# The second layer's small products moved from two quarters of TensorE to all four, with the values scaled ahead

## The reference, cut to what matters

```python
q = q / (norm(q) + EPS);  k = k / (norm(k) + EPS)          # per head, 64 wide
def step(s, inp):                                           # s: 64 x 64 per image and head
    qt, kt, vt, at, bt = inp
    s = s * at[..., None]
    u = einsum('bhd,bhdv->bhv', kt, s)
    s = s + bt * (kt[..., None] * (vt - u)[..., None, :])
    out = einsum('bhdv,bhd->bhv', s, qt)
y = y * rsqrt(mean(y * y, axis=-1) + EPS) * head_norm_w     # per head
```

## Time and profile before

| | |
|---|---|
| median of 3 runs | 722.4 us (719.88 to 723.09) |
| the profiled execution | 720.78 us, its span 719.0 us |
| PE busy | 633.8 us (88%) |
| DVE, ACT, POOL busy | 331.9, 268.5, 143.8 us |
| granted PE clock, mean | 0.938 |

### The profile page before, as it was taken

How to read it: one execution, slowest core, us unless ns; L and a number is a source line. 1 busy time by engine, 2 the same in 40 slices (tenths; PEclk the granted TensorE clock), 3 DMA queues, 4 the chain that set the end, 5 groups by cost and what they waited for, 6 DMA issues and landing times.

```text
span 719.0 us, 20213 instructions
## 1 busy us (share of the span) xinstructions
PE 633.8 (88%) x9154; PEld 468.0 (65%) x9154; DVE 331.9 (46%) x519; ACT 268.5 (37%) x536; POOL 143.8 (20%) x125
## 2 busy tenths in 40 slices
PE   8976497883899997679999998889999999999997
PEld 5654495682799996465566555665599966555553
DVE  0495835730011110374777778769636752411311
ACT  0353232210323232125566665457644533111223
POOL 9101020013000001712445445600043200000000
PEclk9987678985999999599999999999999999999999
DMA  9200000008998870100000020100000070000001
GB/s 316 106 0 2 4 3 2 1 5 303 406 346 312 337 277 29 52 0 24 26 26 26 27 83 20 45 4 0 2 4 5 5 293 1 1 0 1 0 1 45
DMA packets 20229, 56.38 MB, mean 78 GB/s; under 512 B 4272, under 2 KB 13104, under 8 KB 15792
## 3 DMA queue, kind: packets, MB, share of 16 engines
q1 hardware_dynamic: 19376, 53.00, 20.1%
q0 software_dynamic: 768, 2.10, 0.9%
HBM read 49.57 MB, written 5.52 MB: 77 GB/s over the span
## 4 chain that ended last, share of the span: by engine, by line
PE 70%; DVE 15%; issue 4%; ACT 4%; DMA 3%; POOL 2%; SPq 2%; DVEq 0%; ACTq 0%; POOLq 0%
PE PS L1461 8%; PE PS L1429 6%; PE PS L1501 6%; PE PS L1418 6%; PE PS L1597 6%; PE PS L610 4%; PE PS L1627 3%; PE PS L568 3%; PE PS L1604 3%; PE PS L600 3%; PE PS L578 3%; PE PS L589 3%; PE PS L1310 2%; PE PS L1324 2%; PE PS L249 2%
## 5 line engine op out<-in xcount | busy, mean ns | idle before, releaser
L1461 PE MATMUL PS<-Y,arena 128*128 128x392 f32 x192 | 75.1, 521 | 3.9 <-ACT Y L1190 3.9
L1501 PEld LDWEIGHTS PS<-arena 64*49 64x49 f32 x3584 | 50.8, 124 | 36.6 <-issue 22.2
L1501 PE MATMUL PS<-arena 64*49 64x48 f32 (+2 forms) x3584 | 57.3, 213 | 10.3 <-DVE arena L1749 5.7
L1418 PE MATMUL PS<-arena 128*128 128x128 f32 x448 | 54.8, 283 | 4.0 <-DMA arena<-in_moe_b 3.4
L1418 PEld LDWEIGHTS PS<-arena 128*128 128x128 f32 x448 | 54.2, 199 | 5.6 <-DMA arena<-in_moe_b 4.0
L1744 DVE COPY_PREDICATED arena<-msk,PS 128x768 f32<-128x768 int32 x24 | 44.9, 1870 | 27.3 <-PE PS L1501 27.3
L1184 ACT ACTIVATE arena<-PS,arena 128x128 f32<-128x128 f32 x112 | 31.8, 369 | 64.9 <-PE PS L1418 64.9
L1122 POOL TENSOR_TENSOR arena<-arena 128x384 f32<-128x384 f32 (+1 forms) x32 | 37.7, 1179 | 83.2 <-PE PS L1501 79.5
L1429 PE MATMUL PS<-arena 128*128 128x256 f32 x224 | 50.5, 379 | 0.0
L1461 PEld LDWEIGHTS PS<-Y,arena 128*128 128x128 f32 x192 | 33.9, 192 | 23.9 <-ACT Y L1190 4.2
L392 POOL TENSOR_TENSOR arena<-arena,work 128x512 f32<-128x512 f32 x20 | 25.4, 1270 | 114.0 <-DVE work L700 114.0
(11 more groups left out here) (226 smaller groups left out, 1133.9 us busy)
## 6 DMA issues: line engine op xcount, KB each, us to landing
arena<-in_moe_w SPq DMA_DIRECT2D x28, 1024.0 KB, 6.3
arena<-in_qka_w SPq DMA_DIRECT2D x8, 384.0 KB, 3.0
arena<-in_patches SPq DMA_DIRECT2D x6, 392.0 KB, 5.7
arena<-in_ff_w SPq DMA_DIRECT2D x1, 2048.0 KB, 7.7
arena<-in_ffn_w SPq DMA_DIRECT2D x2, 1024.0 KB, 12.6
by_expert<-arena SPq DMA_DIRECT2D x1, 1792.0 KB, 11.2
arena<-in_moe_b SPq DMA_DIRECT2D x14, 128.0 KB, 7.4
arena<-by_expert SPq DMA_DIRECT2D x14, 128.0 KB, 5.8
```

The lines of the kernel that those rows point to most:

```text
L1418: m = nc.tensor.matmul(PS[:, 4 + 2 * (j % 2) + f // 4, (f % 4) * P:(f % 4 + 1) * P], MW1[j % NW][:, k, f * P:(f + 1) * P], XT[:, j % 2, k] ...
L1461: m = nc.tensor.matmul(bank(i % 3), GW[g % 2][:, k, u // 2], half(Y[:, k], u % 2), start=(k == 0), stop=(k == KT - 1))
L1501: m = nc.tensor.matmul(o, K[r, b, :], v, start=True, stop=True)
```

## The change

Six things change:

1. Layer 2 (`PARTS = 2`): for odd pairs the matrices A, PT and U of an image lie on the other half of the partitions than its values. `small` writes them there (`c_`), `pe_rows` and `act_out` follow. A small product of an odd pair thus goes through a quarter of PE whose rows are one half and whose columns are the other, and a product of all 16 walks over all four quarters (`product`). Layer 1 keeps `PARTS = 1` and its two quarters.
2. In both layers a product now takes two banks at once (even pairs in one, odd pairs in the other), so each of the four has one buffer of two banks instead of two of one.
3. The values are multiplied by the key length ahead, head by head, on POOL (L395 of the changed kernel), when all values are stored. Then z is subtracted by DVE straight out of PSUM (L727), and POOL's subtraction and DVE's multiplication fall away.
4. The scaling of y goes from DVE to POOL (L399).
5. ACT masks only the second block of A; POOL clears the first block (L389).
6. `pe_rows` of layer 2 uses 64x49 quarters too, 8 rows in a group instead of 4; the squares, sums and roots come an iteration later.

```diff
-            def pool_apply(self, pool):
-
+            def pool_apply(self, pool, values_kept):
+
+                self.wait(pool, "turned_in", self.totals()["turned_in"])
+                nc.gpsimd.memset(self.Am[:, :, 0:BL], 0.0).then_inc(self.s["a_cleared"], 1)
+                self.wait(pool, "lengths", self.n_lengths)
+                pool.wait_ge(*values_kept)
                 for h in range(self.nh):
-                    self.wait(pool, "z_kept", h + 1)
                     w = self.W[:, :, h * DH:(h + 1) * DH]
-                    nc.gpsimd.tensor_tensor(w, w, self.ZT[h % 2], ALU.subtract).then_inc(self.s["w_kept"], 1)
+                    key = root[:, self.S + h * BP:self.S + (h + 1) * BP].unsqueeze(2).broadcast_to([P, BP, DH])
+                    nc.gpsimd.tensor_tensor(w, w, key, ALU.mult).then_inc(self.s["w_scaled"], 1)
+                for j in range(self.nh // 2):
+                    self.wait(pool, "y_inv", j + 1)
+                    y = self.y(j)
+                    nc.gpsimd.tensor_tensor(y, y, self.sums(y_var, j).unsqueeze(3).broadcast_to([P, BP, 2, DH]),
+                                            ALU.mult).then_inc(self.s["y_done"], 1)
...
+            def product(self, i, operands, back=False):
+
+                for pair in range(0, BP, 2):
+                    for b in (pair, pair + 1):
+                        for cc in range(2):
+                            there = (cc + b) % 2 if self.PARTS == 2 else cc
+                            r, o = (there, cc) if back else (cc, there)
+                            lhsT, rhs = operands(self.part(r), b)
+                            m = nc.tensor.matmul(
+                                PS[self.part(o), 2 * i + b % 2, (b // 2) * DH:(b // 2 + 1) * DH], lhsT, rhs,
+                                start=True, stop=True)
+                return m
...
                     if h < self.nh:
-                        if h >= 2:
-                            self.wait(pe, "d1_kept", h - 1)
-                        for b in range(BP):
-                            for cc in range(2):
-                                r = self.part(cc)
-                                m = nc.tensor.matmul(PS[r, h % 2, b * DH:(b + 1) * DH], self.U[r, h, b, :],
-                                                     self.W[r, b, h * DH:(h + 1) * DH], start=True, stop=True)
-                        m.then_inc(self.s["d1_mm"], 1)
+                        self.wait(pe, "w_scaled", h + 1)
+                        if h:
+                            self.wait(pe, "d1_kept", h)
+                        self.product(0, lambda r, b: (self.U[r, h, b, :], self.W[r, b, h * DH:(h + 1) * DH])) \
+                            .then_inc(self.s["d1_mm"], 1)
...
-                        nc.vector.tensor_tensor(
-                            self.ZT[h % 2], PS[:, 2 + h % 2, :].rearrange("p (b v) -> p b v", b=BP),
-                            inv_k[:, h * BP:(h + 1) * BP].unsqueeze(2).broadcast_to([P, BP, DH]),
-                            ALU.mult).then_inc(self.s["z_kept"], 1)
+                        nc.vector.tensor_tensor(self.head(h), self.head(h), self.result(1), ALU.subtract) \
+                            .then_inc(self.s["w_kept"], 1)
...
                         for b in (2 * pair, 2 * pair + 1):
-                            o = PS[TP * (b % 2):TP * (b % 2) + T, pb + hd]
+                            c_ = (b + pair) % 2
+                            o = PS[TP * c_:TP * c_ + T, pb + hd]
...
-            delta1.pool_apply(pool)
+            delta1.pool_apply(pool, (v1_kept, 2 * BP))
```

More of the change, by code:

```diff
@@ L516, in act_mask @@
                 self.wait(act, "turned_in", self.totals()["turned_in"])
-                nc.scalar.activation(self.Am, self.Am, ACT.Copy, scale=c("first")).then_inc(self.s["a_masked"], 1)
+                second = self.Am[:, :, BL:T]
+                nc.scalar.activation(second, second, ACT.Copy, scale=c("first")).then_inc(self.s["a_masked"], 1)
             def act_out(self, act, g):
@@ L557, in pe_apply @@
                 self.wait(pe, "a_masked", 1)
+                self.wait(pe, "a_cleared", 1)
                 for i in range(self.nh + 5):
@@ L573, in pe_apply @@
                         self.wait(pe, "d1_kept", h + 1)
-                        if h >= 2:
-                            self.wait(pe, "z_kept", h - 1)
-                        for b in range(BP):
-                            for cc in range(2):
-                                m = nc.tensor.matmul(PS[self.part(cc), 2 + h % 2, b * DH:(b + 1) * DH],
-                                                     self.A[self.part(cc), h, b, :],
-                                                     self.D[self.part(cc), h, b, :], start=True, stop=True)
-                        m.then_inc(self.s["z_mm"], 1)
+                        if h:
+                            self.wait(pe, "w_kept", h)
+                        self.product(1, lambda r, b: (self.A[r, h, b, :], self.D[r, h, b, :]), True) \
+                            .then_inc(self.s["z_mm"], 1)
                     h = i - 3
@@ L584, in pe_apply @@
                         self.wait(pe, "w_kept", h + 1)
-                        self.kept(pe, "delta", h - 2)
-                        for b in range(BP):
-                            for cc in range(2):
-                                r = self.part(cc)
-                                m = nc.tensor.matmul(PS[r, 4 + h % 2, b * DH:(b + 1) * DH],
-                                                     self.U[r, h, b, :], self.W[r, b, h * DH:(h + 1) * DH],
-                                                     start=True, stop=True)
-                        m.then_inc(self.s["delta_mm"], 1)
+                        self.kept(pe, "delta", h - 1)
+                        self.product(2, lambda r, b: (self.U[r, h, b, :], self.W[r, b, h * DH:(h + 1) * DH])) \
+                            .then_inc(self.s["delta_mm"], 1)
                     h = i - 5
@@ L595, in pe_apply @@
                         self.kept(pe, "delta", h)
-                        self.kept(pe, "out", h - 2)
-                        for b in range(BP):
-                            for cc in range(2):
-                                r = self.part(cc)
-                                m = nc.tensor.matmul(PS[r, 6 + h % 2, b * DH:(b + 1) * DH],
-                                                     self.PT[r, h, b, :], self.D[r, h, b, :], start=True, stop=True)
-                        m.then_inc(self.s["out_mm"], 1)
+                        self.kept(pe, "out", h - 1)
+                        self.product(3, lambda r, b: (self.PT[r, h, b, :], self.D[r, h, b, :]), True) \
+                            .then_inc(self.s["out_mm"], 1)
                     if 0 <= i - self.nh - 1 < self.EARLY:
```

118 lines of the change are left out of this document (62 added, 56 removed).

## The result

The changed kernel takes 751.0 us (median of 4 runs, 748.16 to 753.38) against 722.4; the ratio is 1.039, 95% interval 1.0354 to 1.0425. The forecast was 717, with a range up to 726. The changed kernel's profiled execution has a span of 751.5 us against 719.0.

The account below looks back on a forecast made before the run. The prediction took PE's products to bound layer 2's apply stage, DVE's dependent instructions the solve stages and hand-offs layer 1's apply stage. -24.0 + 9.8 + 3.6 + 6.1 - 0.6 = -5.1 us gave 717 us, range 704 to 726.

Parts of the forecast that it names:

- What four quarters give: Layer 2's products: 32 records on four quarters of PE take 0.49 us in place of 0.89.
- PE then needs 8 x 0.49 = 3.9 us: Layer 2's apply stage: PE's time for two heads, so that DVE binds and PE sees 4.1 instead of 7.1.
- -24.0: Layer 2's apply stage: forecast change in us, 39.7 in place of 63.7.
- The third rival: Layer 2's products: quarters take turns at the PSUM banks, a product stays at 0.89, 743 us; chance 0.06.
- Rows of A: Layer 2's `pe_rows` behind the last mask: four groups of 64 records, 0.8 us each, and fewer DVE instructions, -0.6 us.
- POOL's clear: Clearing of A's first block: masks and clears were to hide behind the solve chains, at no cost.
- Values scaled ahead, layer 2: End of layer 2's solve chain: POOL and DVE shut each other out for ten DVE instructions, +9.8 us.
- Layer 1: Beginning of layer 1's solve chain: POOL's four multiplications hold DVE up, +3.6 us, bounds 0 and 4.4.
- Layer 1's apply stage: Lost second buffers, POOL's scaling of y and a longer half clock: +6.1 us, bounds 4 and 9.
- DVE's 4.0 to 4.4 us for two heads: Layer 2's apply stage: DVE's work for two heads, which was to bind once the products were faster.
- the slower rival: Layer 2's apply stage: rings of single buffers bind, two heads take 5.4 instead of 4.1, 726 us; chance 0.17.

Follow-up runs that it names:

- the later scaling: Changed kernel, but POOL multiplies the values only after the solve chain in both layers, and ACT masks all of A with no clear by POOL: 737.2 us.
- the half kernel: Changed kernel, but each of layer 2's four products of a head issues only half of its small products: 728.9 us.

## Why the prediction was wrong

- **The step that failed** is "What four quarters give" and what rests on it, "PE then needs 8 x 0.49 = 3.9 us". The duration was right: a product takes 0.50 us inside a burst, and at 15.9 ns a record nothing shows of banks that take turns. The pace was wrong. The step took the array to be all that PE waits for, and left out the supply of instructions. I took the pace from 64 records, half of one packet, and used it for 2048 matmul records in a row. In steady state two heads take 7.0 to 7.6 us, not 4.1; that is the 26.5 us between -24.0 and +2.5. The third rival has the outcome (no gain in the stage, 743 us, chance 0.06), but by banks that take turns, so it would have been right by luck. The trace of the kernel before could have warned me: from 537 us on its iterations take 3.73 to 4.00 us where four products of 0.89 are 3.57, and each pause in them ends 1.2 to 1.6 us after a packet of the instruction queue has landed.
- **Rows of A** failed by the price, "0.8 us each" against 1.9 for a group of 64, and by the count: all six groups, not four, stand behind the last masked product. The price was carried over from other small products; here PE takes four records in 0.119 us without a gap, so it isn't the supply, and the cause of this pace stays open. That is 5.4 of the 7.7; 2.25 are POOL's clear, of which I wrote that it hides. The two make this step the second largest miss, 8.3 us.
- **Values scaled ahead, layer 2**: the mechanism was right, shown by the later scaling. The size was 7.2 for 9.8: one turn costs DVE 0.7 us, not 0.95, since the durations of the ten instructions add up to 11.5 us instead of 4.3. **Layer 1**: the first d1 came 1.8 later against 3.6 forecast, and scaling later gave 2.2 back. POOL's four multiplications take 4.03 us, 1.0 each where I had 1.27.
- **Layer 1's apply stage**: +7.0 for +6.1. Nearly all of it is the single buffers (6.7 back with two). POOL's scaling of y takes 1.9, not 2.5, and matters by less than 1 us here.
- **DVE's 4.0 to 4.4 us for two heads** was right (3.98 in the kernel with half the products), but never came to bind in the changed kernel.
- **Rivals**: the slower rival (rings in layer 2) has the right side and the wrong mechanism; the half kernel rules it out as the main cause. Single buffers alone do cost there too: with two quarters 70.8 us against 64.6 with two buffers, though that pair also differs in y and in the scaling's place.
- **Left open**: the +3.8 us between the layers. Over this stretch the traces of all fourteen kernels, most with the same code there, lie between 358.6 and 363.7 us, so it is scatter of single executions as far as this shows. The last 1.6 us follow a first projection at half clock (4.49 us instead of 2.87), with PE idle much of the time ahead of it; no run isolated that.
